# Attention 0's opening: the key weights in column halves, loads ahead of the key stores, evictions in TensorE's order, a second V tile ahead of the turns of x

## The reference, cut to what matters

```
x = x + tanh(g_xattn[0]) * attention0(layernorm(x), ctx, ctx, mask, Wq, Wk, Wv, ...)   # 16 heads of 32
x = x + tanh(g_ffn[0])   * ffn0(layernorm(x), ...)                                     # 2048 wide
x = x + tanh(g_xattn[1]) * attention1(layernorm(x), ctx, ctx, ...)
x = x + tanh(g_ffn[1])   * ffn1(layernorm(x), ...)

q = heads(x_q @ Wq.T + bq);  k = heads(ctx @ Wk.T + bk);  v = heads(ctx @ Wv.T + bv)
scores = q k^T / sqrt(32) - 10000 * (1 - mask);  out = softmax(scores) v
```

## Time and profile before

| | |
|---|---|
| time, median of 3 runs | 1621.13 us (1617.88 to 1622.68) |
| profiled execution: its time | 1617.83 us |
| profiled execution: span, first to last instruction | 1616.0 us |
| TensorE busy in it | 1576.3 us (98%) |
| mean granted TensorE clock | 0.994 of 2.4 GHz |

### The profile page before, as it was taken

How to read it: one execution, slowest core, us unless ns; L and a number is a source line. 1 busy time by engine, 2 the same in 40 slices (tenths; PEclk the granted TensorE clock), 3 DMA queues, 4 the chain that set the end, 5 groups by cost and what they waited for, 6 DMA issues and landing times.

```text
span 1616.0 us, 25557 instructions
## 1 busy us (share of the span) xinstructions
PE 1576.3 (98%) x9262; PEld 1434.7 (89%) x9262; DVE 1028.0 (64%) x1828; ACT 970.6 (60%) x2006; POOL 391.9 (24%) x540
## 2 busy tenths in 40 slices
PE   6999999999998999999999999999999999999898
PEld 5899899999977999999999998889999989998655
DVE  5477777787786453223544435637777777778886
ACT  4566667677765456454554435347677767766576
POOL 3111211212133222222232222312112120213641
PEclk9999999999998999999999999999999999999999
DMA  7675867676572225555265643576576667657400
GB/s 235 138 191 153 200 167 191 163 194 177 142 201 72 95 88 166 184 176 189 81 227 202 210 169 92 178 173 180 147 201 159 170 168 187 170 142 195 166 13 30
DMA packets 146164, 257.77 MB, mean 160 GB/s; under 512 B 40833, under 2 KB 90113, under 8 KB 145900
## 3 DMA queue, kind: packets, MB, share of 16 engines
q1 hardware_dynamic: 145580, 255.82, 56.0%
q10 hardware_dynamic: 448, 0.14, 0.1%
HBM read 187.49 MB, written 58.57 MB: 152 GB/s over the span
## 4 chain that ended last, share of the span: by engine, by line
PE 90%; DVE 4%; ACT 2%; POOL 2%; issue 1%; DMA 1%; SPq 1%; ACTq 0%; DVEq 0%; POOLq 0%
PE ps L1017 32%; PE ps L718 17%; PE ps L714 15%; PE ps L783 8%; PE ps L771 7%; PE ps L844 2%; PE ps L755 2%; PE ps L760 2%; PE ps L956 1%; PE ps L758 1%; PE ps L759 1%; DMA QT<-in_wv 1%; PE ps L881 1%; DVE hb L1426 1%; DVE nmax L1147 0%
## 5 line engine op out<-in xcount | busy, mean ns | idle before, releaser
L1017 PE MATMUL ps<-ah_f,wh_f 128*128 128x400 f32 (+1 forms) x1296 | 446.2, 345 | 0.9 <-issue 0.8
L1017 PE MATMUL ps<-al_f,wh_f 128*128 128x400 f32 (+1 forms) x1296 | 444.8, 344 | 0.0
L1942 POOL TENSOR_TENSOR cxl<-raw,cxh 128x384 fp32r<-128x384 f32 (+1 forms) x112 | 105.6, 964 | 616.5 <-ACT cxh L1580 616.5
L1513 DVE TENSOR_TENSOR wl_f<-raw_f,wh_f 128x1024 fp32r<-128x1024 f32 x85 | 103.9, 1224 | 235.3 <-POOL wh_f L2162 235.3
L1017 PEld LDWEIGHTS ps<-ah_f,wh_f 128*128 128x128 f32 x1296 | 245.5, 189 | 2.4 <-issue 1.5
L1017 PEld LDWEIGHTS ps<-al_f,wh_f 128*128 128x128 f32 x1296 | 245.8, 190 | 0.0
L1147 DVE TENSOR_REDUCE nmax<-ps 100x1 f32<-100x722 f32 x256 | 220.8, 904 | 32.0 <-PE ps L759 28.6
L1622 ACT ACTIVATE P<-ps,nmax 100x722 f32<-100x722 f32 x256 | 220.2, 862 | 32.5 <-DVE nmax L1147 32.3
L1634 ACT ACTIVATE PT<-ps 128x400 fp32r<-128x400 f32 x384 | 166.2, 505 | 72.6 <-PE ps L771 71.4
L1875 ACT ACTIVATE raw_f<-wl_f 128x1024 f32<-128x1024 f32 x88 | 93.4, 1062 | 175.2 <-DVE wl_f L1513 175.2
L1153 DVE TENSOR_TENSOR PT<-ps,PT 128x400 fp32r<-128x400 f32 x384 | 196.5, 568 | 3.2
(11 more groups left out here) (194 smaller groups left out, 2501.3 us busy)
## 6 DMA issues: line engine op xcount, KB each, us to landing
KS<-kd SPq DMA_DIRECT2D x192, 361.0 KB
raw_f<-in_h SPq DMA_DIRECT2D x64, 512.0 KB, 4.7
raw_f<-in_gud SPq DMA_DIRECT2D x48, 512.0 KB, 4.5
raw<-in_ctx SPq DMA_DIRECT2D x64, 192.0 KB, 4.1
raw_f<-in_w SPq DMA_DIRECT2D x24, 512.0 KB, 3.5
kd<-ksh SPq DMA_DIRECT2D x60, 192.0 KB, 2.2
kd<-ksl SPq DMA_DIRECT2D x60, 192.0 KB, 2.3
raw<-in_ctx SPq DMA_DIRECT2D x64, 169.0 KB, 4.3
```

The source lines that it names most:

```text
L1017: return e.matmul(o, p, q, start=start, stop=stop)
L1513: e.tensor_tensor(wl[:, z, :], raw[:, r, :], raw32(wh[:, z, :]), ALU.subtract).then_inc(v_ul, 1)
L1942: e.tensor_tensor(m.cx[1][:, k, off:off + n], m.raw[:, k, off:off + n], raw32(m.cx[0][:, k, off:off + n]), ALU.subtract).then_inc(g_cx, 1)
```

## The change

In attention 0 (`L == 0`), five things are done:

1. wk is loaded in two halves of its columns. `load_wk` loads columns 0 to 255 of each chunk (groups 0 and 1 of K); columns 256 to 511 of all chunks come in one DMA (`m.wk23`, semaphore `d_wk`) after the context. ScalarE and VectorE split the second halves in new `split_wk` steps.
2. SP issues gt, ident (from ScalarE's queue before), the rest of wk, all of wv, x, wq, mask and x's last four tiles ahead of every store of K (`store_k`), and the mask rows after them.
3. ScalarE and VectorE do K's evictions and the weights' splits in turns: K00, wk's second halves, K01, wv 4 and 5, K10, wv 6 and 7, K11, and so on. wq's splits stand ahead of V0's eviction.
4. TensorE makes V1 before the first two turns of x, and V2 between the first and the second pair of turns, so that `query(0)` follows the second pair directly.
5. GpSimd makes the roots and wq's low parts before the mask rows.

The core of the diff (semaphore bookkeeping left out: `d_wo` and `d_bo` are joined in `d_out`, and the counts of `v_wl` and `a_wh` are four higher from the second halves on):

```diff
                 for k in range(4):
                     load_ctx(L, m, 0, 0, k)
-                    load_w(L, m, k)
+                    if L == 0:
+                        load_wk(m, k)
+                    else:
+                        load_w(L, m, k)
                 for k in range(4):
                     load_ctx(L, m, 0, 1, k)
                 if L == 0:
+                    e.dma_start(gt[:, :], t["g"].partition_broadcast(128)).then_inc(d_const, 16)
+                    e.dma_start(ident[:, :], t["ident"]).then_inc(d_const, 16)
+                    e.dma_start(m.wk23, t["wk0"][:, :, 256:512]).then_inc(d_wk, 16)
+                    load_w(L, m, 4)
...
+                    load_w(L, m, 7)
                     for b in range(4):
                         load_x(m, b)
-                    for i in range(4, 8):
+                    for i in range(8, 12):
                         load_w(L, m, i)
...
+            def load_wk(m, k):
+
+                e.dma_start(m.stage[k][:, 0:256], t["wk0"][:, k, 0:256]).then_inc(d_w[k], 16)
+
             def load_w(L, m, i):
                 if i >= 6:
                     wait_low_w(w, L, i - 6)
+                    if L == 0 and i < 10:
+                        w.wait_ge(v_wl, low_groups(i - 6))
...
                         wait_low_w(w, L, (0 if j[0] == "k" else 4) + k)
+                        if L == 0 and j[0] == "k" and j[2] >= 2:
+                            w.wait_ge(v_wl, low_groups(k))
...
                 for j in (K01, K10, K11, K20, K21, V0):
                     job(j)
+                if L == 0:
+                    job(V1)
                 turn_x(0)
                 turn_x(1)
-                job(V1)
+                job(V1 if L else V2)
                 turn_x(2)
                 turn_x(3)
-                job(V2)
+                if L:
+                    job(V2)
                 query(0)
...
+                def split_wk(k):
+
+                    cs = slice(256, 512)
+                    w.wait_ge(d_wk, 16)
+                    e.activation(m.wk[0][:, k, cs], m.stage[k][:, cs], ACT.Copy).then_inc(a_wh, 1)
```

More of the change, by code:

```diff
@@ L255, in scol @@
             return cols[:, i:i + 1]
-        d_const, d_mask, d_mrow, d_s3, d_wo, d_bo = (
-            sem("d_" + n) for n in ("const", "mask", "mrow", "s3", "wo", "bo"))
+        d_const, d_mask, d_mrow, d_s3, d_out, d_wk = (
+            sem("d_" + n) for n in ("const", "mask", "mrow", "s3", "out", "wk"))
         d_ctx = [[sem(f"d_ctx{h}{k}") for k in range(4)] for h in range(2)]
@@ L424, in wait_low_w, with high_w, low_groups @@
             else:
-                w.wait_ge(v_wl, 10 * L + i + 1)
+                w.wait_ge(v_wl, (14 if L else 4 if i >= 4 else 0) + i + 1)
+        def high_w(L, i):
+            return (16 if L else 4 if i >= 4 else 0) + i + 1
+        def low_groups(k):
+            return 4 + k + 1
         def kst_of(m, b, g):
@@ L473, in attention @@
                 if L == 0:
+                    e.dma_start(gt[:, :], t["g"].partition_broadcast(128)).then_inc(d_const, 16)
+                    e.dma_start(ident[:, :], t["ident"]).then_inc(d_const, 16)
+                    e.dma_start(m.wk23, t["wk0"][:, :, 256:512]).then_inc(d_wk, 16)
+                    load_w(L, m, 4)
+                    load_w(L, m, 5)
+                    load_w(L, m, 6)
+                    load_w(L, m, 7)
                     for b in range(4):
                         load_x(m, b)
-                    for i in range(4, 8):
+                    for i in range(8, 12):
                         load_w(L, m, i)
+                    e.dma_start(m32, t["mask"]).then_inc(d_mask, 16)
+                    for b in range(4, 8):
+                        load_x(m, b)
                     store_k(L, m, *K00[1:])
                     store_k(L, m, *K01[1:])
-                    for b in (4, 5):
-                        load_x(m, b)
                     store_k(L, m, *K10[1:])
-                    for b in (6, 7):
-                        load_x(m, b)
+                    store_k(L, m, *K11[1:])
+                    store_k(L, m, *K20[1:])
+                    store_k(L, m, *K21[1:])
                     for c in range(2):
@@ L487, in attention @@
                         e.dma_start(mrow[:, c, :], raw32(m.KS[0:B, 0, c, :])).then_inc(d_mrow, 16)
[L488 to L492, removed]
                     w.wait_ge(d_mrow, 32)
@@ L1116, in split_w @@
                     k = i % 4
-                    w.wait_ge(a_wh, 12 * L + i + 1)
-                    e.tensor_tensor(wlow[i // 4][1][:, k, :], m.stage[i % 6], raw32(wlow[i // 4][0][:, k, :]),
+                    cs = slice(0, 256 if L == 0 and i < 4 else 512)
+                    w.wait_ge(a_wh, high_w(L, i))
+                    e.tensor_tensor(wlow[i // 4][1][:, k, cs], m.stage[i % 6][:, cs], raw32(wlow[i // 4][0][:, k, cs]),
+                                    ALU.subtract).then_inc(v_wl, 1)
+                def split_wk(k):
+                    cs = slice(256, 512)
+                    w.wait_ge(a_wh, 4 + k + 1)
+                    e.tensor_tensor(m.wk[1][:, k, cs], m.stage[k][:, cs], raw32(m.wk[0][:, k, cs]),
                                     ALU.subtract).then_inc(v_wl, 1)
@@ L1304, in attention @@
                     low_job(K00)
-                    for i in range(4, 8):
-                        split_w(i)
+                    for k in range(4):
+                        split_wk(k)
                     low_job(K01)
+                    split_w(4)
+                    split_w(5)
+                    low_job(K10)
+                    split_w(6)
+                    split_w(7)
+                    low_job(K11)
                     stats_x(0)
                     stats_x(1)
-                    low_job(K10)
+                    low_job(K20)
                     stats_x(2)
                     stats_x(3)
-                    low_job(K11)
-                    low_job(K20)
                     low_job(K21)
+                    split_w(8)
+                    split_w(9)
                     for b in range(4):
@@ L1354, in attention @@
                     stats_x(b)
[L1355 removed]
+                if L:
+                    low_job(V2)
                 for b in range(4, len(IN[L])):
@@ L1711, in attention @@
                     high_job(K00)
-                    for i in range(4, 8):
+                    for k in range(4):
+                        split_wk(k)
+                    high_job(K01)
+                    split_w(4)
+                    split_w(5)
+                    high_job(K10)
+                    split_w(6)
+                    split_w(7)
+                    high_job(K11)
+                    high_job(K20)
+                    high_job(K21)
+                    for i in range(8, 12):
                         split_w(i)
-                    for j in (K01, K10, K11, K20, K21):
-                        high_job(j)
                 else:
@@ L1721, in attention @@
                 high_job(V0)
+                if L == 0:
+                    high_job(V1)
                 turned_x(0)
                 turned_x(1)
[L1724 to L1727, removed]
+                high_job(V1 if L else V2)
                 turned_x(2)
                 turned_x(3)
-                high_job(V2)
+                if L:
+                    high_job(V2)
                 high_query(0)
@@ L2069, in attention @@
                 if L == 0:
-                    w.wait_ge(v_cx, 8)
+                    input_roots(0)
+                    low_wq(10)
+                    low_wq(11)
                     w.wait_ge(d_mask, 16)
```

29 lines of the change are left out of this document (13 added, 16 removed).

## The result

The changed kernel takes 1623.9 us, the median of 20 runs (1618.91 to 1627.21), beside 1618.98 us of the kernel before in 20 runs on the same chip. The ratio is 1.0026 with a 95% interval of 1.0017 to 1.0035: **slower**, by 4.2 us on 1619 (the two medians lie 4.9 us apart; what follows goes by the recorded ratios, which are not the quotients of the medians). The forecast was 3.1 us faster, and the time lies above the range. The profiled execution took 1624.95 us, its span was 1623.2.

What follows compares the result with a forecast made beforehand. TensorE, busy 1576.3 of 1616.0 us, was taken as the bound. 3.9 + 1.6 + 1.0 - 1.85 - 1.5 = 3.15, taken as 3.1 us faster: 1621.13 to 1618.0 us, range 1614.5 to 1623.0, widened by a us at each end.

Steps and rivals of the forecast that it cites:

- The start: Opening loads: half chunks of wk put fewer bytes ahead of the context; 1.0 us gained, bounds 0 and 1.8.
- The stall ahead of K11: TensorE's 3.92 us idle before K11 goes away; K11 at full clock saves another 1.6 us.
- K20 and K21: Jobs after K11: K20 covered by 0.7 us; K21 covered by 0.5 us or short by 0.8, by wv's landing.
- Rival A: Whole opening: lead larger, 5 to 7 us, from a fuller start, earlier clock rise, quick x chain; chance 0.22.
- B: Gated wv chunks land late at K21: 0.8 us lost (chance 0.05), or 1625.2 us (0.08, shared with late SP).
- C's late wk: K11 waits for wk's second half, landing 3 us later (17.5), so the stall only moves: 1620.0 us; no separate chance.
- V0 to `query(0)`: Stretch where the change gives back: new waits of 1.5 us ahead of V2 and 1.85 us ahead of `query(0)`.
- roots on GpSimd, 26.95 to 30.56 = 3.6 us: In x's chain ahead of V2, GpSimd's roots take 3.6 us as before, ending at 29.2.
- four scalings, 1.91: In x's chain ahead of V2, VectorE's four scalings of x take 1.91 us as before, ending at 31.1.
- 0 for all of them: Remaining edits (K's stores, mask rows, wq's low parts, gt and ident on SP) cost 0, up to 1 us loss.
- whether 2.2 or 2.5 us are enough to lose it no row shows: Around V2 and `query(0)`, stretches of only transposes and waits might drop the clock, costing 1.6 us each time.
- rival C's fall: Clock falls once in the new gaps around V2 and `query(0)`, giving 1619.6 us; chance 0.20.

Runs made afterwards that it cites:

- e1: Changed kernel, with GpSimd's wq low parts and mask rows held until VectorE has scaled x's first four tiles; 1618.9 us, ratio 0.9998 to the kernel before.
- e2: Changed kernel, with only the mask rows held behind the scalings of x, wq's low parts left beside them; 1622.79 us, ratio 1.0018 to before.
- e4: Changed kernel, GpSimd's wq and mask work behind the scalings, V1 back between the turn pairs and V2 ahead of `query(0)`; 1618.12 us, ratio 0.9988 to before.
- f2: Changed kernel, with useless transposes (29, 14 and 16 of 128 columns) in TensorE's three waits; 1621.34 us, ratio 1.0014 to before.
- e3: Changed kernel, with VectorE's low parts of V0 and V1 ahead of the scalings of x; 1621.46 us, ratio 1.001 to before.
- e5: Kernel before, with eight useless GpSimd multiplications of a scratch tile behind the roots, beside VectorE's scalings; 1618.12 us, ratio 1.0.
- g3: Changed kernel, GpSimd's wq and mask work behind the scalings, V0's low part ahead of them, both turn pairs between V1 and V2; 1615.12 us, ratio 0.997.
- f1: Changed kernel, with useless matmuls (16, 8 and 9 of 384 columns) in TensorE's three waits; 1622.05 us, ratio 1.001 to before.
- g1: Changed kernel, GpSimd's work behind the scalings, turns between V1 and V2, x loaded ahead of wv 6 and 7, statistics tile by tile; 1617.77 us, ratio 0.9988.

## Why the prediction was wrong, by its steps

**The start** was put at 1.0 us with 1.8 as its bound; it is larger: the first matmul starts 2.5 us earlier (5.21, before 7.75), K10 3.1 us earlier (13.87, before 17.00), and K11 starts at 15.98, where 18.3 was forecast. **The stall ahead of K11** is gone as forecast, with its clock: no row of TensorE waits there. wk's second half was there at 12.74, not 14.5. **K20 and K21:** a wait of 0.35 us, between the 0 and 0.8 of the text. V0's start at 22.57 beats the forecast of 24.1 by 1.5 us. Rival A was right so far; no part of B or of C's late wk happened in this execution. The place is as thin as the text says: of the seven other profiles with these loads, K21 waited 1.42 us in e1, 1.43 in e2 and 1.09 in e4, and under 0.6 in the rest.

**V0 to `query(0)`** failed, in three terms:

1. *"roots on GpSimd, 26.95 to 30.56 = 3.6 us"*: 4.7 us (24.22 to 28.94), since wq's low parts on VectorE now lie beside them.
2. *"four scalings, 1.91"*, and with it *"0 for all of them"* for GpSimd's moved work. This is the step that fails first and costs most. I asked only who waits for that work, not what it stands beside. It cost 3.6 us: 5.47 with it, 1.92 without (e1). V0's low part was ready at 35.0, where the text has 31.8. The Trainium skill ("SBUF — State Buffer", "🔬 SBUF: two separate sides") states that VectorE, in some of its operations, and GpSimd share a pair of ports under a lock held for a whole instruction, and that the one that doesn't have it stops. The traces agree, at 1.92 us with nothing on GpSimd and 2.82 to 5.47 with something, each scaling ending 0.3 us behind a GpSimd instruction. It could have been asked ahead of the prediction. The mask rows moved from 15.55, ahead of the roots, to behind wq's low parts. And the low parts themselves, the dearer piece by e2, had only waited for wq's cast on ScalarE, which the earlier loads bring forward: they start at 28.89 instead of 36.60, with the scalings. The prediction doesn't follow them.
3. *"whether 2.2 or 2.5 us are enough to lose it no row shows"*: the clock was lost. That is rival C's fall, which I priced at 1.6 us and gave 0.20. It cost about 2.4 us on V2 and 1.7 on `query(0)`; the turns' wait had grown to 3.39 us, and three waits stood close together. In e1, with the scalings quick and waits of 1.45 and 0.95 us ahead of V2, it still fell for part of V2 (4.25 us instead of 2.8). The 1.69 us ahead of e1's `query(0)` cost nothing: it took 9.01 us. So the forecast of 1.5 us idle at V2 with no cost in clock would probably not have held even without the first error, and that of 1.85 at `query(0)` probably would have. No run has just those waits.

The last term, **1.85 us in front of `query(0)`**, was right: 1.69.

Summed from the forecast's 37.3: V0's low part 3.2 later (35.0 against 31.8; the roots began 1.4 earlier than forecast, and took 1.1 and the scalings 3.6 longer), 2.4 for V2's clock and about 0 for the last wait: 42.9, and the profile has 42.87. The 1.7 us of `query(0)`'s own clock come on top: 7.3 us worse than the forecast, which was 3.1 faster. That is 4.2 slower. The lead at V0 doesn't enter this sum, because V2 waits for x's chain and not for TensorE.

The *rule against the sum* went wrong in its reason. The clock did fall, but not because the turns don't count: with transposes in the waits (f2) it stayed at 1.00. The Trainium skill's sentence ("TensorE: Matmul & The Clock Gate", "Part 4: PE-mode transpose"), that transposes don't count as busy for the gate, isn't borne out by f2 for these f32 transposes. TensorE's standing still was the cause.

How far the opening sets the time can be read from the start of the turns behind `query(0)` less 49.34, beside the ratio's us:

| kernel | by the opening | by the ratio |
|---|---|---|
| after | +4.15 | +4.2 |
| e2 | +2.9 | +2.9 |
| e3 | +1.7 | +1.6 |
| e1 | -0.8 | -0.3 |
| e5 | -0.7 | 0.0 |
| e4 | -1.7 | -1.9 |
| g3 | -4.0 | -4.9 |
| f1 | -0.45 | +1.6 |
| f2 | -0.2 | +2.3 |
| g1 | -4.0 | -1.9 |

Seven agree within a us. The last three are 2 to 2.5 us above, at the edge of intervals of about 2 us each way or just outside them (f2's begins at +0.6). Whether something behind the opening costs them that, no run settles.

## What to carry to other kernels

When work is moved off the path on GpSimd or VectorE, look at what the other of the two does at its new place: here a scaling of 0.54 us took up to 2.68, and a root step of 1.05 took 2.16, because each stood until the other engine's instructions beside it were done. It is the length of those instructions that counts, and TensorE pays it whole when it waits for that chain. A lead ahead of a join is worth only as much as the slowest input of the join has gained; here TensorE gained 8 us and x, which V2 and `query(0)` need, lost. Several waits of 1 to 3 us close to each other cost TensorE between a third and a bit over a half as much again in clock (4.1 us for 7.3 in the changed kernel, 1.5 for 4.1 in e1, 1.1 for 2.2 in g3). A job that lies ready, such as V2, is best put where it covers a wait that must come.

## What was not expected of the hardware

GpSimd's reciprocal root step on 100 x 4 numbers takes 1.05 us alone and 2.16 beside two subtractions of 128 x 512 on VectorE. The subtractions lay at 24.50 to 25.79 and the step ended 0.90 us later, so it stood through nearly all of them. A tiny operation is stretched like a large one.

How long TensorE runs at the lower level behind the opening differs from execution to execution, with the same instructions in the same order: from 60 us on it is 8.5 us in f2's profile and 28.2 in f1's, counted from the granted clock of its stretches. Their spans are 1615.6 and 1621.4 us though their openings end within 0.3 us of each other. Runs of one kernel spread over some 8 us likewise, and their granted clock goes with it: of g3's runs one took 1618.24 us at a mean of 0.989, another 1610.15 at 0.999. So a single profiled span can't be compared here at this size; the opening's rows and the ratios over many runs can.
